# Turning the gathered rows of sixteen experts by DMA transposes in place of TensorE, in a macaron block (expert layer, attention, expert layer)

## The reference, cut to what matters

```python
logits = jnp.einsum('bsd,ed->bse', hidden_states, gate_w)
scores = jax.nn.softmax(logits, axis=-1).transpose(0, 2, 1)
topk_w, topk_idx = jax.lax.top_k(scores, cap)          # 16 experts, cap = 256 tokens per sequence
x_tok = jnp.take_along_axis(hidden_states[:, None, :, :], topk_idx[..., None], axis=2)
g = jnp.einsum('becd,efd->becf', x_tok, Wg)            # 256 -> 512
u = jnp.einsum('becd,efd->becf', x_tok, Wu)
h = jax.nn.gelu(g, approximate=False) * u
eo = jnp.einsum('becf,edf->becd', h, Wd) * topk_w[..., None]
flat = flat.at[flat_idx].add(eo.reshape(-1, d))        # and a shared expert is added on all tokens
```

## Time and profile before

| | us |
|---|---|
| median of 3 runs (lowest, highest) | 1521.3 (1519.48, 1523.49) |
| profiled execution, first to last instruction | 1516.2 |
| what lies around it: median less that span | 5.1 |
| TensorE busy in the profiled execution | 1481.7 |
| ScalarE, VectorE, GpSimd busy | 973.5, 899.3, 556.4 |

### The profile page before, as it was taken

One profiled execution on the slowest core, in us unless ns is written; L12 is line 12 of the kernel. 1 busy time (PEld: TensorE's weight loads), 2 busy tenths in 40 slices (PEclk: granted clock), 3 DMA queues, 4 the chain that ended last, 5 costly groups with the idle time before them and its releaser, 6 DMA issues. The chain is left out here.

```text
span 1516.2 us, 26897 instructions
## 1 busy us (share of the span) xinstructions
PE 1481.7 (98%) x10085; PEld 1041.7 (69%) x10085; DVE 899.3 (59%) x2012; ACT 973.5 (64%) x1335; POOL 556.4 (37%) x500
## 2 busy tenths in 40 slices
PE   5999999999999999999999999999999999999998
PEld 4788888888997763333343333333788898888887
DVE  7888776666667971222144052036887967666674
ACT  7322354454535889999999999999622244445442
POOL 5000356666646971111111021120300046666645
PEclk9999999999999999999999999999999999999999
DMA  8312366666636799505336163122412256666653
GB/s 302 77 56 70 100 182 147 157 147 155 170 65 167 263 278 182 86 1 86 58 85 128 40 117 62 25 70 70 146 56 70 70 157 154 147 157 147 163 120 42
DMA packets 122162, 181.06 MB, mean 119 GB/s; under 512 B 19056, under 2 KB 84080, under 8 KB 119280
## 3 DMA queue, kind: packets, MB, share of 16 engines
q1 hardware_dynamic: 93856, 131.61, 33.1%
q0 software_dynamic: 28176, 47.73, 15.6%
HBM read 123.73 MB, written 55.57 MB: 118 GB/s over the span
## 5 line engine op out<-in xcount | busy, mean ns | idle before, releaser
L2446 ACT ACTIVATE 6417_pr<-6417_pS 128x1024 f32<-128x1024 f32 x448 | 420.5, 1191 | 2.9 <-PE 6417_pS L2338 2.9
L2369 PE MATMUL 6417_pO<-6417_pr,6402_vres 128*32 128x512 f32 x1792 | 238.1, 605 | 0.0
L2338 PEld LDWEIGHTS 6417_pS<-sq_rows,sk_rows 50*128 50x128 f32 x896 | 77.5, 184 | 180.0 <-ACT 6417_pr L2446 132.5
L2338 PE MATMUL 6417_pS<-sq_rows,sk_rows 50*128 50x512 f32 x896 | 184.1, 469 | 2.3 <-issue 1.3
L351 PE MATMUL 6428_pGU<-columns_ahead,weights_wts 128*128 128x512 f32 (+1 forms) x400 | 155.4, 388 | 0.2 <-DVE 6428_hf L1246 0.2
L352 PE MATMUL 6428_pGU<-columns_ahead,weights_wts 128*128 128x512 f32 (+1 forms) x400 | 152.6, 381 | 0.0
L353 PE MATMUL 6428_pGU<-columns_ahead,weights_wts 128*128 128x512 f32 (+1 forms) x400 | 152.4, 381 | 0.0
L2470 POOL TENSOR_SCALAR_AFFINE_SELECT 6417_pr<-6417_pr 128x512 f32<-128x512 f32 x32 | 20.6, 643 | 358.6 <-ACT 6417_pr L2446 358.6
L1070 ACT ACTIVATE hidden_hT<-93_hf 128x512 fp32r<-128x512 f32 x96 | 60.7, 632 | 141.6 <-DVE 93_hf L1246 141.6
L1070 ACT ACTIVATE hidden_hT<-6428_hf 128x512 fp32r<-128x512 f32 (+1 forms) x100 | 61.5, 615 | 138.1 <-DVE 6428_hf L1246 138.1
L1510 POOL DMA_INDIRECT out<-eo,6428_idx x64 | 109.2, 1706 | 95.9 <-issue 67.0
(11 more groups left out here) (438 smaller groups left out, 3583.4 us busy)
## 6 DMA issues: line engine op xcount, KB each, us to landing
93_raw_g<-WgT SPq DMA_DIRECT2D x16, 512.0 KB, 4.0
93_raw_u<-WuT SPq DMA_DIRECT2D x16, 512.0 KB, 3.6
93_raw_d<-WdT SPq DMA_DIRECT2D x16, 512.0 KB, 4.4
q_rows<-rows_halves SPq DMA_DIRECT2D x8, 1024.0 KB, 5.3
k_rows<-rows_halves SPq DMA_DIRECT2D x8, 1024.0 KB, 5.1
6428_raw_g<-WgT SPq DMA_DIRECT2D x16, 512.0 KB, 3.9
6428_raw_u<-WuT SPq DMA_DIRECT2D x16, 512.0 KB, 3.7
6428_raw_d<-WdT SPq DMA_DIRECT2D x16, 512.0 KB, 4.0
```

Source lines behind the costliest of these rows:

```text
L2338: m = t_.matmul(to[:, e, :], key, query, start=True, stop=True)
L2369: m = t_.matmul(pO[e * 32:(e + 1) * 32, j % 2, off:off + wd], vres[:, (g // GB) * TPB + kt, at:at + 32], from_(e), start=n == first[j], st ...
L2446: s_exp.done(a.activation(to, pS[:, u % RING, :, :], ACT.Exp, scale=HD ** -0.5))
```

## The change

It concerns the fifteen experts after the first in each layer. ScalarE (`part_planes`) copies a gathered item's 512 x 256 float32 values as 16-bit integers into `planes`: for each of the four groups of 128 rows, first the lower halves of all 256 values and then the upper ones. SyncE issues four DMA transposes (`turn_planes`), each of 128 rows x 512 halves, into `turned_planes`. ScalarE (`join_planes`) interleaves the halves again, one Copy for each 128 inputs, into `joined`, and copies that to the high part. VectorE (`lower`) makes the low part in one instruction of 1024 elements. TensorE's `turn` is left for the first expert alone. The three routing buffers and the new ones share one region of memory, and the gather's wait for the turn becomes a wait for the parting.

```diff
--- before.py
+++ after.py
...
@@ -472,6 +472,7 @@
             wts = [weights_at[k]("wts", [P, 6, DC * F], f32r) for k in range(2)]
             if lead:
                 wts += [columns_at[h]("wts", [P, 6, DC * F], f32r, 8 * KB) for h in range(2)]
+            joined = columns_at[1]("joined", [P, 2, DC, W], f32)
             xn_all = weights_at[0]("xn", [P, KN, 4, D], f32)
             hT = [hidden_at(f"hT{h}", [P, 2, FC, W], f32r, 16 * KB * h) for h in range(2)]
             xq_all = hidden_at("xq", [P, J, 4, D], f32)
@@ -482,7 +483,10 @@
             xr = t.sb("xr", [P, 2, 4, ROW])
             wt = t.sb("wt", [P, 2, 4])
             scores = t.sb("scores", [P, 4, B, 4, E])
-            rows = t.sb("rows", [P, 4, P])
+            routing_at = region("routing", 10 * KB)
+            rows = routing_at("rows", [P, 4, P], f32)
+            planes = routing_at("planes", [P, 4, 2 * D], self.u16)
+            turned_planes = routing_at("turned_planes", [P, 2, DC, W], self.u16, 4 * KB)
             idx = t.sb("idx", [P, E, B, CAP // P], self.i32)
             st6, mv = t.sb("st6", [P, 2, 4, 6]), t.sb("mv", [P, 2, 4, 2])
             std, rstd, shift = (t.sb(n_, [P, 2, 4]) for n_ in ("std", "rstd", "shift"))
@@ -562,6 +566,7 @@
                 sig("dve_" + n_) for n_ in ("stats", "mv", "rstd", "shift", "xl", "soft", "rows", "mul", "hl", "ev", "wl", "wt",
                                             "dif", "cnt", "route", "go", "hot", "idx"))
             s_wls, s_whs = sig("pool_wl"), sig("pool_wh")
+            s_planes, s_planes_turned, s_joined = sig("planes"), sig("planes_turned", 64), sig("act_joined")
             lowered = lambda n: 2 * n - (4 if ready else 0)
             left = lambda q: q - 2 if ready and q < 5 else q - 1
             s_Dq, s_evq = sig("pe_last_D"), sig("dve_last_ev")
@@ -577,12 +582,12 @@
...
-            gt, eq, sel = (t.sb(n_, [P, B, TPB, E], bf16) for n_ in ("gt", "eq", "sel"))
+            gt, eq, sel = (routing_at(n_, [P, B, TPB, E], bf16, (2 + k) * KB) for k, n_ in enumerate(("gt", "eq", "sel")))
...
@@ -760,6 +765,14 @@
                 def load_residual(d):
                     s_so[d % 2].wait(sp, d // 2)
                     s_res[d % 2].done(sp.dma_start(eo[:, d % 2, :, :], xv[d]))
+
+                def turn_planes(item):
+                    s_planes.wait(sp, item - J)
+                    s_joined.wait(sp, DC * (item - J - 1))
+                    for q in range(4):
+                        s_planes_turned.part(sp.dma_start_transpose(
+                            turned_planes[:, :, :, q * P:(q + 1) * P].rearrange("p h c t -> p (h c) t"),
+                            planes[:, q, :]), 16)
 
                 for q in range(J):
                     if q >= first and not ready:
@@ -793,8 +806,10 @@
                 load_weight(1, 1)
                 load_weight(1, 2)
                 for e in range(2, E):
+                    turn_planes(J + e - 1)
                     for w in range(3):
                         load_weight(e, w)
+                turn_planes(NI - 1)
                 if lead:
                     self.load_projection_weights(sp)
                     s_wl.wait(sp, 3 * E)
@@ -954,8 +969,6 @@
                 def turn(item, c):
                     if c == 0:
                         s_rows[item % 2].wait(t_, (item - J) // 2 + 1)
-                    if item > J:
-                        s_xl.wait(t_, lowered(item - 1) + c + 1)
                     for q in range(4):
                         m = t_.transpose(turned(c)[:, q * P:(q + 1) * P], xr[:, item % 2, q, c * P:(c + 1) * P], self.ident[:, :])
                     s_T.done(m)
@@ -999,9 +1012,6 @@
                             down(s, 0)
                             down(s, 1)
                         gu(s, 1)
-                    if s < NI:
-                        turn(s, 0)
-                        turn(s, 1)
                     if s > NI:
                         last_down(NI - 1)
                     elif s > J + 1 and not (lead and s == NI):
@@ -1041,6 +1051,22 @@
                     a.wait_ge(*s_LT.at(q + 1))
                     for c in range(DC):
                         s_xh.done(a.activation(XT[0][:, q, c, :], pT(q, c), ACT.Copy))
+
+                def part_planes(item):
+                    s_rows[item % 2].wait(a, (item - J) // 2 + 1)
+                    s_planes_turned.wait(a, item - J - 1)
+                    halves = xr[:, item % 2, :, 0:D].bitcast(self.u16).rearrange("p q (d h) -> p q h d", h=2)
+                    s_planes.done(a.activation(planes[:, :, :].rearrange("p q (h d) -> p q h d", h=2), halves, ACT.Copy))
+
+                def join_planes(item):
+                    n, col = item - J, column(item)
+                    s_planes_turned.wait(a, n)
+                    s_U.wait(a, 4 * (item - 1))
+                    for c in range(DC):
+                        s_joined.done(a.activation(joined[:, col, c, :].bitcast(self.u16).rearrange("p (t h) -> p t h", h=2),
+                                                   turned_planes[:, :, c, :].rearrange("p h t -> p t h"), ACT.Copy))
+                    s_joined.wait(a, DC * n)
+                    s_xh.part(a.activation(XT[0][:, col, :, :], joined[:, col, :, :], ACT.Copy), DC)
 
                 def gathered(item):
                     s_U.wait(a, 4 * (item - 1))
@@ -1117,6 +1143,8 @@
                         continue
                     if s == J + 1:
                         gathered(J)
+                    if J < s < NI:
+                        part_planes(s)
                     if J < s < NI - (2 if lead else 0):
                         split(s, 0)
                         split(s, 1)
@@ -1133,7 +1161,7 @@
                     if J - 3 <= s < J:
                         split(J, s - J + 3)
                     if J < s < NI:
-                        gathered(s)
+                        join_planes(s)
                     if J < s < NI - (2 if lead else 0):
                         split(s, 2)
                     if lead and s == NI - 3:
@@ -1250,6 +1278,12 @@
                     n, cut = number(s, f, h), piece_of(h)
                     v.wait_ge(*s_hh.at(n + 1))
                     s_hl.done(v.tensor_tensor(hT[1][:, i % 2, f, cut], hf[:, f % 2, cut], hT[0][:, i % 2, f, cut].bitcast(f32), ALU.subtract))
+
+                def lower(item):
+                    col = column(item)
+                    v.wait_ge(*s_xh.at(2 * (item + 1)))
+                    s_xl.part(v.tensor_tensor(XT[1][:, col, :, :], joined[:, col, :, :], XT[0][:, col, :, :].bitcast(f32),
+                                              ALU.subtract), DC)
 
                 def gathered(item):
                     for c in range(DC):
@@ -1358,7 +1392,7 @@
                     if s == NI - 2:
                         split(s + 1, 0)
                     if s < NI:
-                        gathered(s)
+                        lower(s)
                         if s < NI - 1:
                             split(s if s == NI - 3 else s + 1, 1)
                         evacuate(s, 0)
@@ -1479,7 +1513,9 @@
                 def gather(item):
                     k, e = item % 2, item - J
                     if e >= 2:
-                        s_T.wait(g, 2 * (e - 1))
+                        if e == 2:
+                            s_T.wait(g, DC)
+                        s_planes.wait(g, e - 2)
                         s_wt.wait(g, e - 1)
                     self.settle(g)
                     for q in range(4):
```

More of the change, by code:

```diff
@@ L294, in __init__ @@
         self.f32, self.f32r = mybir.dt.float32, mybir.dt.float32r
-        self.bf16, self.f16, self.i32 = mybir.dt.bfloat16, mybir.dt.float16, mybir.dt.int32
+        self.bf16, self.f16, self.i32, self.u16 = mybir.dt.bfloat16, mybir.dt.float16, mybir.dt.int32, mybir.dt.uint16
         self.ACT, self.ALU, self.AX = mybir.ActivationFunctionType, mybir.AluOpType, mybir.AxisListType
@@ L583, in ffn @@
             in_group = t.sb("in_group", [P, B, NTG, E], bf16)
-            hi, lo = t.sb("hi", [P, B * TE], bf16), t.sb("lo", [P, B * TE], bf16)
-            own = t.sb("own", [P, B, NG, WQ, G])
+            hi, lo = (routing_at(n_, [P, B * TE], bf16, (5 + k) * KB) for k, n_ in enumerate(("hi", "lo")))
+            own = routing_at("own", [P, B, NG, WQ, G], f32, 7 * KB)
             found = t.sb("found", [P, B, NG, 2, G])
```

## The result

The changed kernel takes 1664.2 us (median of 4 runs, 1660.03 to 1665.68) against 1521.5 us for the kernel before, run beside it: a ratio of 1.0938 (95% interval 1.0925 to 1.0952). It is slower by 142.7 us. Forecast was 1606, with a range of 1553 to 1760: the sign and the range held, the size came out 58 us over the forecast.

A forecast was written before the change was run, and what follows sets the result against it. TensorE was taken to bound the kernel before at 17.53 us per item, and the ScalarE-VectorE chain, 19.0 us, after. 1521.3 + 47 (chain and late gate load) + 38 (transposes landing late) = 1606 us, range 1553 to 1760.

The forecast's parts named there:

- What is removed: On TensorE, 240 of 256 transposes go, 30 items by 0.79 us: 23.7 us, the whole gain there can be.
- Copies of 16 bits: On ScalarE, parting and joining cost as other Copies: 1.90 us for 2048 elements, 1.04 for 1024.
- The rival of Copies at twice the rate: ScalarE's 16-bit Copies run twice as fast, chain 17.0 us, about 1506 us if transposes land early; chance 0.04.
- The chain: ScalarE and VectorE work from one step's last hidden part to the next's: 18.96 us, where TensorE needs 16.74.
- Every us beyond 5.55 goes into the chain as it is: From parting's end to joining, 5.55 us are covered; each us beyond lengthens the chain, in some 26 of 30 items.
- the wait of TensorE's part 0 for mul 2: TensorE's next-step up product of part 0 waits for VectorE's mul 2 to free its bank, about 2.3 us per item.
- The landing: Four DMA transposes land 7.0 us after the parting, 1.45 over their cover: 26 x 1.45 = 38 us.
- First steps have room: First steps, like the first layer's end, have room, so late transposes there do not lengthen the chain.
- The load at the first layer's end: The last expert's gate load stands behind item 22's transposes and lands about 417.8 against 415.71: 2 us.
- The clock: A fall of TensorE's granted clock at its new gaps would add to the time; no size given.
- transposes hidden: Rival: the DMA transposes land within 5.55 us, the chain stays 19.0: 1568 us; chance 0.30.
- in series: Rival: each DMA transpose works alone, 15.6 us to land: 1829 us; chance 0.15 for more than 12 us.

The follow-up runs named there:

- The last experiment: Changed kernel with `lower` late, parting one item early, TensorE turning each layer's first two experts, first layer's last load ahead of the last transposes: 1504.5 us.

## Why the prediction was right, and where it was not

- **What is removed** was right: 240 matmuls less, 23.7 us at most. The last experiment shows what they are worth when most of the rest is hidden, 16.3 us for 28 items; where the other 6 us went was not followed to the end.
- **Copies of 16 bits** were taken as other Copies. The parting was to take 1.90 us and takes 1.89. The joins were to hold the list 0.95 and 1.04 us and take 2.26 together: interleaving from two planes costs 1.17 us for 1024 elements against 1.04. That is 0.3 us per item, 9 us in all, which the sum lacked. The rival of Copies at twice the rate is out.
- **The chain** was the step that the forecast rested on, and it held. 18.96 us forecast, 0.3 for the joins, is 19.3; without transposes an item took 19.25. With the shown item's landing of 7.32, the first join at 9.74 (1415.80 to 1425.54) and not at 7.98, it gives 18.96 + 1.76 + 0.3 = 21.02; measured 21.06. By layers: the forecast's chain costs near 21 and 24.2, each with 4.5 for the joins near 25.5 and 28.7; the kernel without transposes is longer than the kernel before by 25.6 and 29.5. (The 2 us for the late gate load are not in this: without transposes it does not come late.)
- **Every us beyond 5.55 goes into the chain as it is**: right. The 4.48 us wait ahead of `lower` and the wait of TensorE's part 0 for mul 2 (1.73 us, forecast 2.3) are where the prediction put them.
- **The landing** is the term that was mis-sized: 7.0 us forecast, three issues of 0.82 and 3.9 behind them and 0.6 for the busy queues. Measured on the shown item: three issues of 1.27 on the mean and 3.19 behind. The row that I took for an issue, a store of 512 short rows, was not near enough: an issued transpose holds SyncE half as long again. On the shown item the longer issues and the shorter transfer nearly cancel, 7.32 against 7.0; over all items the mean is 7.87 and 8.41 in the two layers (second, first). There the 0.6 for sharing was too small, since holding back the gathers alone gave 1.3 per item. In the second layer, 14 x (7.87 - 5.55) = 32.5 and 5.3 for the first item; in the first 12 x (8.41 - 5.55) = 34.3 and 5.3. The first layer's last two items have their own cover, 7.41 and 3.65 us, as the kernel without transposes shows, so that 12.99 and 6.30 cost 5.6 (the late gate load) and 2.6. So the landing cost 80.0 where 38 stood, and the gate load 5.6 where 2 stood. Together 85.6. The difference between the kernels with and without transposes, in the two layers, is 46.7 and 38.9: 85.6.
- **"First steps have room"** was wrong. Both first items waited 5.2 to 5.3 us, longer than any other item. Over 3 us of that came from the gathers beside them, as the run that held these back shows: there the two waits are 1.87 and 1.95 us.
- **The load at the first layer's end** comes late by the mechanism that was forecast, a parting, four issues and then the load, but by 5.6 us and not 2: the four issues took 5.50 us (478.25 on), where the sum had 3.3, and the load landed 6.4 us after its issue (483.79 to about 490.2), where the sum had 3.9.
- **Not in the forecast**: 1.9 us ahead of the first layer's experts and 4.65 between the layers. Both are there without transposes too (2.2 and 5.1), and the first also where TensorE turns every item. What causes them was not tried. The second is absent in all four kernels with `lower` late or the parting early (-1.0, 0.0, 0.0 and -0.95 us at the same marks).
- **The clock** fell, which the prediction had allowed for as something that would add to the time. It did not add: items at a mean clock of 0.89 and of 1.00 follow the same rule.

Of the rivals: transposes hidden, 1568, is what would have come without the landing (1581.8 measured, with the joins and the 7 us outside the steps); in series is out, since landings were 6.3 to 11.6 us and not 15.6.

Of the two pages named in the prediction, the first did not hold as a sum over blocks. The Trainium skill (VectorE: DVE Perf Modes, The three transpose paths) has 1309 ns for one block of 128 x 128; 16 such blocks in one transfer landed within 5.5 us here, where 20.9 would be their sum (an estimate by that page), and four transfers of four blocks landed in 6.3 to 9.3 in the second layer behind its first item. The same Trainium skill (Advanced Engine Details and Errata, X-Bar Transpose (TRN2)) has them as fast as regular DMAs. For the issue that did not hold: 512 KB took one issue of 0.60 us as a load and 5.21 us of issues as four transposes, or 2.02 as one. For the transfer no run compares like with like: a transpose of 128 KB landed 3.19 us after the start of its issue, and a load of 512 KB takes 3.9.

## What to carry to other kernels

Price what a moved operation does to the lists behind it, and not to its engine's busy share: ScalarE was busy for 64% before and took 1.9 us more per item at no cost, while 2.95 us of each item came from one VectorE instruction that stood ahead of others and had become late. A DMA transpose must be paid per transfer on the queue that issues it, so few large ones are cheaper (1602.3 in place of 1664.2), and it can be started a whole step early. With four small ones, but started early, with `lower` moved back and one more item per layer left to TensorE, the same idea gave 1504.5. Large transfers on top of that were not tried. Then look at the ends, since what repeats may be hidden and the first and last items still cost 22 us (1526.7 against 1504.5).

## What the runs showed of the hardware that I had not expected

- A DMA transpose holds SyncE for 1.27 us (median of 120; 1.19 to 2.23) for 4 blocks of 128 x 128 halves, and for 2.03 us for 16 blocks (median of 30; 1.32 to 5.14).
- Indirect gathers beside them lengthen the landing, some 1.3 us per item by the run that held the gathers back, and not the issues, whose four took 5.46 and 5.49 us on the mean with and without.
- The 16 DMA engines at a share of 0.87 to 0.90 for 100 us did not keep TensorE from being busy all the time; in the changed kernel they stood at 0.95 to 0.99 while transposes were under way.
- Around a wait of 1.73 us TensorE's clock went to 1.2 GHz for some 6 us (1412 to 1418), and the item took what its landing gives, as items at the full clock do.
- A Copy that joins two planes of 16-bit halves takes 1.15 to 1.19 us for 1024 elements, where a float32 Copy takes 1.04; the parting, with a stride of two, takes 1.89 to 1.91 for 2048, where the float32 rows gave 1.90.
